# A graph network layer: edge sums kept transposed, and the node's own part multiplied in the edge stage

## What is computed

```python
h = jnp.maximum(_layernorm(x, axis=-1), 0.0)
# inside the first layer, with self loops of zero edge attributes added:
e = jax.nn.relu(ea @ ee_w1 + ee_b1) @ ee_w2 + ee_b2
msg = x[src] + e
agg = jax.ops.segment_sum(msg, dst, num_segments=n)
h = (1.0 + eps) * x + agg
h = jax.nn.relu(_ln(h @ w1 + b1, g1, be1))      # 256 -> 1024
h = jax.nn.relu(_ln(h @ w2 + b2, g2, be2))      # 1024 -> 1024
y = h @ w3 + b3                                 # 1024 -> 256
```

## Time and profile before

| | |
|---|---|
| median of 3 runs | 3159.45 us (3154.38 to 3160.02) |
| span of the profiled execution | 3157.3 us |
| block prepare | 0 to 93.0 us |
| block edges0 | 93.0 to 1107.8 us |
| block nodes, its steady part | 1250 to 2020 us |
| mean granted TensorE clock | 0.906 |

### The profile page before, as it was taken

How to read it: one execution, slowest core, us unless ns; L and a number is a source line. 1 busy time by engine, 2 the same in 40 slices (tenths; PEclk the granted TensorE clock), 3 DMA queues, 4 the chain that set the end, 5 groups by cost and what they waited for, 6 DMA issues and landing times. The chain is left out here.

```text
span 3157.3 us, 79016 instructions
## 1 busy us (share of the span) xinstructions
PE 2446.9 (77%) x25310; PEld 2164.9 (69%) x25311; DVE 2156.6 (68%) x3833; ACT 1488.6 (47%) x3803; POOL 1976.9 (63%) x2143
## 2 busy tenths in 40 slices
PE   0577777777777789999999999947777777777763
PEld 0466666666666679999999999945555555555552
DVE  7676667777677636666666666657766766666666
ACT  5444444444444458888888888831111111111114
POOL 4677777777777634444444444437777777777772
PEclk9998889999899889999999999978888888887996
DMA  6555555555555500000000000026555655555554
GB/s 158 168 161 149 158 154 166 161 163 160 159 164 158 143 25 18 21 21 20 20 21 20 20 22 21 21 61 178 171 173 173 174 172 168 173 172 173 171 170 136
DMA packets 183839, 373.69 MB, mean 118 GB/s; under 512 B 42598, under 2 KB 93688, under 8 KB 183769
## 3 DMA queue, kind: packets, MB, share of 16 engines
q0 software_dynamic: 75552, 209.66, 23.5%
q1 hardware_dynamic: 107392, 162.37, 17.4%
q10 hardware_dynamic: 824, 0.87, 0.1%
HBM read 346.95 MB, written 25.80 MB: 118 GB/s over the span
## 5 line engine op out<-in xcount | busy, mean ns | idle before, releaser
L446 POOL DMA_INDIRECT rows<-tab_scratch,srcs x784 | 765.7, 977 | 238.7 <-issue 234.1
L1458 POOL DMA_INDIRECT a_rows<-tab_scratch,srcs x784 | 750.5, 957 | 251.7 <-issue 235.8
L1524 PE MATMUL sum_ps<-feat,a_hot 128*125 128x264 f32 x1960 | 601.5, 463 | 237.5 <-DVE feat L1616 121.0
L1524 PEld LDWEIGHTS sum_ps<-feat,a_hot 128*125 128x125 f32 x1960 | 417.4, 222 | 341.7 <-DVE feat L1616 133.9
L876 PE MATMUL z_ps<-ah,w 128*128 128x125 f16 x6400 | 553.8, 219 | 1.0 <-PEq L982 1.0
L876 PE MATMUL z_ps<-al,w 128*128 128x125 f16 x3200 | 542.7, 217 | 0.0
L876 PEld LDWEIGHTS z_ps<-ah,w 128*128 128x128 f16 x6400 | 489.5, 97 | 1.5 <-issue 1.4
L1468 ACT ACTIVATE feat<-d 128x32 f32<-128x32 f32 x196 | 44.9, 229 | 827.0 <-DVE d L1612 566.2
L500 PE MATMUL mlp_ps<-ewa,eab 128*128 128x256 f16 x788 | 203.5, 290 | 284.3 <-PEq L496 283.3
L478 ACT ACTIVATE rh<-mlp_ps 128x1024 f16<-128x1024 f32 x196 | 199.7, 1019 | 358.2 <-ACTq L477 347.7
L829 POOL TENSOR_TENSOR a<-a 128x500 f32<-128x500 f32 x100 | 124.4, 1244 | 372.1 <-POOLq L828 372.1
(11 more groups left out here) (211 smaller groups left out, 5422.8 us busy)
## 6 DMA issues: line engine op xcount, KB each, us to landing
ea<-edge_t SPq DMA_DIRECT2D x394, 128.0 KB
dstb<-dst_flat SPq DMA_DIRECT2D x98, 512.0 KB
rows<-tab_scratch,srcs POOLq DMA_INDIRECT x784
a_rows<-tab_scratch,srcs POOLq DMA_INDIRECT x784
tab_scratch<-prow SPq DMA_DIRECT2D x50, 128.9 KB
hx<-x SPq DMA_DIRECT2D x50, 125.0 KB
x_scratch<-x SPq DMA_DIRECT2D x50, 125.0 KB
hs<-tab_scratch SPq DMA_DIRECT2D x50, 125.0 KB
```

Source lines behind the costliest of these rows:

```text
L446: pool.indirect_dma_start(rows[:, b % DEEP, k, :], None, dram["tab0"], bass.IndirectOffsetOnAxis(ap=srcs[:, c:c + 1], axis=0),).then_inc(r ...
L1458: pool.indirect_dma_start(rows[:, b % DEEP, k, :], None, dram["tab1"], bass.IndirectOffsetOnAxis(ap=srcs[:, c:c + 1], axis=0),).then_inc(r ...
L1524: ins = pe.matmul(out[:], hot[:, h, k, :], feat[:, row, k, :], start=(k == 0), stop=(k == CB - 1))
```

## The change

`acc` is kept transposed: features in the 128 partitions, and for each tile four blocks of 125 columns, two of the node's features and two of the edge activations.

In edges0 the operands of the sums trade places: the gathered rows and `rh`, `rl` become the weights and `hot` is streamed, 32 products of 125 columns in place of 16 of 256. `hot` is built by four TENSOR_SCALAR instructions of 125 columns from a float16 row in SBUF in place of one SCALAR_TENSOR_TENSOR of 500 columns with its row in PSUM. Once in four batches SP loads one tile's own rows of `tab0` back (`load_own`), PE transposes them with four products into `own_ps`, and DVE adds them, times (eps + 2), to `acc` (`add_own`). PE's loop covers 12 batches in place of 6.

In prepare `own` is gone; `acc` is filled with constants by two POOL copies of 6250 columns and two ACT instructions of 6250 columns, the normalised x goes to another buffer, and ACT's order of `high` and `normalised` is changed.

In nodes `turn`, `turned`, `turnable` and the two identity products are gone. `make_h` is four products that read `acc` directly; it stands behind the first layer. DVE adds the node's own part (`add_own`, into the new SBUF tile `hs`), and `high_h` and `low_h` read `hs` in place of PSUM.

```diff
@@ prepare
             for c in range(CH):
                 pool.wait_ge(norm_ready, c + 1)
                 if c >= 2:
-                    pool.wait_ge(t_free, c - 1)
+                    pool.wait_ge(tb_ready, c - 1)
@@ prepare, ACT
-            for c in range(CH + 2):
-                if c >= 2:
-                    high(c - 2)
+            for c in range(CH + 1):
                 if c < CH:
                     deviation(c)
+                if c >= 1:
+                    high(c - 1)
+                if c < CH:
                     normalised(c)
@@ prepare, DVE
-            for c in range(CH + 2):
-                if c >= 2:
-                    low(c - 2)
-                if 1 <= c < CH:
-                    own(c - 1)
+            for c in range(CH + 1):
                 if c + 1 < CH:
                     stats(c + 1)
+                if c >= 1:
+                    low(c - 1)
+                if c + 1 < CH:
                     coefficients(c + 1)
-            own(CH - 1)
@@ edges0
-    at = dsts[:, bass.ds(CB * (b + 1), CB)].unsqueeze(2).broadcast_to([P, CB, TN])
-    return dve.scalar_tensor_tensor(out=out, in0=at, scalar=negbase[:, bass.ds(tile, 1)],
-                                    in1=iota_ps.unsqueeze(1).broadcast_to([P, CB, TN]),
-                                    op0=ALU.add, op1=ALU.is_equal)
+    for k in range(CB):
+        ins = dve.tensor_scalar(out[:, k, :], iota16[:], dsts[:, bass.ds(CB * (b + 1) + k, 1)], negbase[:, bass.ds(tile, 1)],
+                                ALU.subtract, ALU.is_equal)
@@ edges0, PE
+                    node = hot[:, h, k, :]
+                    for f in range(KD):
+                        pe.matmul(mine, rows[:, ring, k, hi], node, start=(k == 0 and f == 0), stop=False, skip_group_check=True)
+                        pe.matmul(mine, rows[:, ring, k, lo], node, start=False, stop=False, skip_group_check=True)
+                        pe.matmul(edge, rh[:, s, k, hi], node, start=False, stop=False, skip_group_check=True)
+                        ins = pe.matmul(edge, rl[:, s, k, hi], node, start=False, stop=(k == CB - 1 and f == KD - 1), skip_group_check=True)
@@ nodes, PE
+                    for k in range(KD):
+                        edge = acc[:, bass.ds(i, 1), (KD + k) * TN:(KD + k + 1) * TN].rearrange("p a c -> p (a c)")
+                        ins = pe.matmul(h_ps[:, j, :], w2e[:, k, f], edge, start=(k == 0), stop=(k == KD - 1))
@@ nodes, ACT
-                act.wait_ge(h_done, 1)
-                act.sem_inc(h_done, -1)
-                act.activation(hh[:], h_ps, ACT.Copy, scale=1.0 / WS).then_inc(hh_ready, 1)
+                act.wait_ge(hs_ready, 1)
+                act.sem_inc(hs_ready, -1)
+                act.activation(hh[:], hs[:], ACT.Copy, scale=1.0 / WS).then_inc(hh_ready, 1)
@@ nodes, DVE
+            def add_own(i):
+                dve.wait_ge(h_done, 1)
+                dve.sem_inc(h_done, -1)
+                mine = acc[:, bass.ds(i, 1), 0:KD * TN].rearrange("p a c -> p (a c)")
+                dve.tensor_tensor(hs[:].rearrange("p k n -> p (k n)"), h_ps.rearrange("p k n -> p (k n)"), mine, ALU.add).then_inc(hs_ready, 1)
...
-                dve.scalar_tensor_tensor(out=hl[:], in0=h_ps, scalar=1.0 / WS, in1=hh[:],
+                dve.scalar_tensor_tensor(out=hl[:], in0=hs[:], scalar=1.0 / WS, in1=hh[:],
                                          op0=ALU.mult, op1=ALU.subtract).then_inc(h_split, 1)
```

More of the change, by code:

```diff
@@ L168, in _ @@
                 for rows in splits:
-                    sp.dma_start(acc[rows, tiles(c), 0:D], x_v[rows, tiles(c), :]).then_inc(ld_x[c], 16)
+                    sp.dma_start(xbuf(c)[rows], x_v[rows, tiles(c), :]).then_inc(ld_x[c], 16)
             sp.dma_start(sb["srcs"][:], t["src_cols"]).then_inc(stored, 16)
@@ L516, in _ @@
             edge_mlp(0)
+            pe.wait_ge(ident_ready, 1)
+            own()
             def body(tiles, i, u):
@@ L520, in body @@
                 edge_mlp(1 - s)
+                if u % RING == 1:
+                    own()
                 lo, end = tiles[u]
@@ L531, in body @@
                         pe.sem_inc(xhot_ready, -1)
-                        sums(sum_ps[:, 2, :], 2, u, s).then_inc(xsum_done, 1)
+                        sums(sum_ps[:, 2, :], 2, u % DEEP, s).then_inc(xsum_done, 1)
             with pe.Fori(0, FULL) as i:
-                tiles = tiles_of(nc, PE, table, DEEP * i, DEEP)
-                for u in range(DEEP):
-                    body(tiles, i, u)
-            tiles = tiles_of(nc, PE, table, DEEP * FULL, REST)
+                for half_round in range(2):
+                    tiles = tiles_of(nc, PE, table, ROUND * i + DEEP * half_round, DEEP)
+                    for u in range(DEEP):
+                        body({DEEP * half_round + u: tiles[u]}, i, DEEP * half_round + u)
+            tiles = tiles_of(nc, PE, table, ROUND * FULL, REST)
             for u in range(REST):
@@ L615, in _ @@
             low_parts(0)
+            add_own(NT - 1)
             def turn(i):
@@ L714, in nodes @@
         z_ps = [m.ps(f"z{j}_ps", [P, 2, 512]) for j in (1, 2)]
-        tv_ps = m.ps("tv_ps", [P, 3, TN])
-        hv_ps = m.ps("hv_ps", [P, 3, TN])
+        vv_ps = m.ps("vv_ps", [P, 2, TN])
+        h_ps = m.ps("h_ps", [P, KD, TN])[:]
         y_ps = m.ps("y_ps", [P, D])
         gp_ps = m.ps("gp_ps", [P, 512])
-        t_ps, h_ps, v_ps = tv_ps[:, 0:KD, :], hv_ps[:, 0:KD, :], [hv_ps[:, KD, :], tv_ps[:, KD, :]]
+        v_ps = [vv_ps[:, j, :] for j in range(2)]
         g_ps = gp_ps[:, 0:KD * TN].rearrange("p (k n) -> p k n", n=TN)
@@ L969, in body @@
                     layer1(1, range(3, 4))
+                if has(i, 0, 1):
+                    make_h(i + 1)
                 if has(i, 4):
@@ L1076, in body @@
             def body(i, p):
-                if has(i, 0, 1):
-                    turned(i + 1)
                 if has(i, 0):
@@ L1243, in body @@
                 if has(i, 0):
-                    inverse(0, v1_read if has(i, 0, 1) else None)
+                    inverse(0)
                 if has(i, 3):
```

210 lines of the change are left out of this document (108 added, 102 removed).

## The result

| | before | changed |
|---|---|---|
| median | 3159.45 us | 3309.72 us (3304.62 to 3311.61) |
| ratio | | 1.0478 (95%: 1.0464 to 1.0493) |
| span of the profiled execution | 3157.3 us | 3309.8 us |
| first to last of POOL's gathers in edges0 | 94.1 to 1097.4: 1003.3 | 100.8 to 1200.7: 1099.9 |
| last gather of edges0 to first of edges1 (nodes) | 1017.2 | 1063.0 |

The change costs 150 us. The three stages take +6.7 (all before the first gather), +96.6 and +45.8 us; the profiled spans differ by 3.4 more, behind the first gather of edges1, in code that did not change. I had forecast +44: +6, +9 and +29.

A forecast was written before the change was run, and what follows sets the result against it. POOL's indirect DMA gathers were taken to bound edges0, PE the nodes, and a chain of waits prepare. Nodes +29, edges0 +9 and prepare +6 made +44 on the 3159.45 us median: 3203 us, range 3183 to 3225.

The forecast's parts named there:

- The step that failed: edges0: the added PE, DVE and SP work hides behind POOL while DVE and PE stay under 5.2 us a batch.
- Two sizes in the same part: edges0: four `hot` instructions of 0.2 add DVE 0.1 us a batch or less; 50 own-row additions at about 0.42.
- Rival D: edges0 is the larger loss, by `hot` costing POOL as L547 does or PE refetching its loop; 3243, chance 0.07.
- PE has 270 us of air: edges0: PE's spare time, named against PE losing time by refetching instructions in its longer loop.
- six batches of slack: edges0: POOL's slack, named against the edge stage becoming the larger loss.
- The port term, +9,: edges0: new `hot`, SBUF to SBUF, lengthens POOL's issues by 0.009 for each of 984; +9 us, bounds 0 and +37.
- Nodes, +29 forecast: nodes: `low_h` with two SBUF inputs waits for POOL's L829; 0.60 a tile over 48 tiles, bounds -32 and +68.
- the removed products: nodes: two transposes and two identity products gone from PE, worth 0.67 a tile.
- Prepare, +6 forecast: prepare: ACT's new order starts the last rows at 85.3, not 79.13; +6 us, bounds 0 and +10.

The follow-up runs named there:

- experiment 5: Changed kernel with PE's edges0 loop back at 6 batches and without the own rows in edges0 (no load, products or addition): 3236.51 us, ratio 1.0246.
- experiment 6: Changed kernel, PE's edges0 loop of 6 batches, no own rows in edges0, `hot` again one instruction with its row in PSUM: 3205.35 us, ratio 1.0142.
- experiments 1: Changed kernel with PE's loop in edges0 back to 6 batches by an inner loop of two halves, same work and order: 3282.21 us, ratio 1.0386.
- experiment 7: Changed kernel with PE's edges0 loop of 6 batches and `hot` as one SCALAR_TENSOR_TENSOR with its row in SBUF: 3242.26 us, ratio 1.0259.
- experiment 8: Kernel before with the new four-instruction `hot` and one more DVE instruction of 250 columns in each fourth batch of edges0: 3221.17 us, ratio 1.0183.
- experiment 3: Kernel before with PE's loop of 24 batches instead of 6, nothing else changed: 3160.80 us, ratio 1.0004.
- experiment 9: Changed kernel with `h` kept in PSUM in nodes: own part added into `h_ps` in place, `high_h` and `low_h` read PSUM: 3279.47 us, ratio 1.0379.
- experiments 4: Kernel before with the new `hot`, four TENSOR_SCALARs from a float16 row in SBUF, nothing else: 3184.04 us, ratio 1.0071.

## Why the prediction was wrong

**The step that failed** is in the edges0 part: "All of this hides behind POOL as long as DVE and PE stay under POOL's 5.2 us a batch." I took DVE's 718 busy of 1015 us as 300 us of air and costed the new `hot` and `add_own` on DVE at nothing. DVE's gaps are no air. It works in turn with PE and ACT within a batch, and most of its idle time in edges0, 254 of 296 us, is waits for them: for the high parts of the edge attributes (L547) and of the activations (L579), both ACT's, and for PE's sums (L556). Of the kernel before, as totals with number of waits and the longest:

```profile
DVE eab L547 <- DVEq L546: 122.8, 80, 3.6
DVE acc L556 <- DVEq L554: 102.2, 68, 5.0
DVE rl L579 <- DVEq L578: 29.2, 39, 2.5
```

Two pairs of runs that differ in `hot` alone, and have no refetch on DVE, show that its time costs. Between experiments 5 and 6, without the own rows, 66 us of work cost 31. Between experiments 1 and 7, beside the own rows, 64 cost 40, or 55 by POOL's wait. In the changed kernel DVE was 794 us busy of 1112, still far from full. The own rows cost 44, as experiment 5 shows; that DVE's part in them is what costs is argued and not shown, since experiment 8 has the refetch in it and PE's four products weren't tried alone.

A part of each price may be the lower clock. PE's granted clock has two levels in these traces, full (1.00) and half (0.50). Two products of 125 columns start 0.10 us apart in a stretch at 0.50, and 0.05 apart in one at 1.00:

```profile
600.21 0.31 PE L526 MATMUL sum_ps<-hot,rows 128*128 128x125 f16 x1
600.31 0.31 PE L527 MATMUL sum_ps<-hot,rows 128*128 128x125 f16 x1
...
605.15 0.22 PE L526 MATMUL sum_ps<-hot,rows 128*128 128x125 f16 x1
605.20 0.22 PE L527 MATMUL sum_ps<-hot,rows 128*128 128x125 f16 x1
```

Added up over all products between the first and the last gather, the lower level lengthened PE's work by about 106 us in the changed kernel and 82 in the one before; experiments 1, 5 and 6 have 113, 92 and 83. So some 24 of the 97 us could have come by this way. No run held the clock, and whether it falls because PE is kept waiting, or PE's partners are late because it falls, is open.

**Two sizes in the same part.** The four small instructions take about 1.0 together, not 0.8: 243.5 us for 984, which put 68 us on DVE, some 0.3 a batch and not 0.1. And `add_own` is 0.47, not 0.42.

**Rival D** had the stage right and both reasons in a shape that does not hold. `hot` did not cost POOL as L547 does (978 against 977). The refetch is real, 133 packets, but experiment 3 has it at no price. It costs 27 us only beside the rest of the change. I had named both "PE has 270 us of air" and "six batches of slack" against it; only the second held, and only while DVE could catch up. D's chance of 0.07 was far too low, as was its price of 40.

**The port term, +9,** should have been 0. The means are 977 before and 978 after. The form of `hot` that does reach POOL's issues is the one with two SBUF inputs, 976 to 997 in experiment 7. The Trainium skill, "SBUF — State Buffer", section "Who interferes with whom", counts tensor_scalar among the forms that can take the shared ports, and infers that tensor_tensor, with two inputs, leaves descriptor generation alone. The runs show the reverse of what I had drawn from it: no effect of this tensor_scalar that can be seen, and a clear one of a two-input form. Here the measurement decides.

**Nodes, +29 forecast, +45.8 measured.** The mechanism is the one forecast, and experiment 9 shows it: 0.60 a tile from the collision. The period was nearly right, 19.65 against 19.71, with luck: two sizes offset each other, for the removed products are worth 0.48 and not 0.67, and PE's wait is 1.13 and not 1.27. 48 x 0.66 = 32 of the 45.8 are the steady tiles. The other 14 lie at the block's ends: from the last gather to the first `hh` it is 25.4 us where it was 17.7, and the rest is in the first tiles. Without the own rows and with the old `hot` those 25.4 are 16.4 (experiment 6). So these 7.7, about half of the 14, are edges0's lag carried over.

**Prepare, +6 forecast, +6.7 measured, by another way.** I held that ACT's first rows, 4 us later, would be covered by the wait for a stored slot. They start at 26.34, 7.6 later than in the earlier trace rows, and that wait is gone: the rows of ACT follow at 6.71 from there without it, and the last start at 86.95, 7.8 after 79.13. From the first rows to the last it is 60.6 us where it was 60.4. So it is the delay that arrives, and the new order of `high` adds next to nothing to it; no run takes the two apart. DVE's casts show where the delay comes from, one held by each of POOL's two copies:

```profile
8.49 5.50 DVE L263 CAST iota<-icol 128x125 f16<-128x125 int32 x1 [0.24 <-DVEq L252]
14.13 5.17 DVE L264 CAST negbase<-ineg 128x50 f32<-128x50 int32 x1
```

## What to carry to other kernels

Busy share is not slack. An engine that works in turn with others within an iteration can be at 70% and have little time to give. Look at who ends its waits, and if it is its partners in the ring, give added work a price: here 66 us of it cost 31, and 64 cost 40 where more had been added beside it. A stall that a deep buffer swallows (here 5 us at a loop's back edge) comes back as soon as the stages behind it can't catch up, so an edit that is free alone can be dear beside another. Compare the instruction queues of an experiment too, engine by engine: two runs here, made to isolate DVE's work, brought a refetch on DVE of their own. And move work to a stage in which its engine is idle: the own rows cost 44 us in edges0, and with them in prepare, in place of POOL's fills, prepare became 5.8 us shorter.

## What the hardware showed

- PE's loop of 24 batches of the old form, or of 12 of the new one, was fetched anew in each round (103 and 133 packets on the instruction queue; 27 to 30 with shorter loops), at about 3 us more for a back edge (5.50 against the 2.4 to 3.0 of a table load alone).
- DVE's loop was fetched anew in experiments 4 and 8 alone (100 and 99 packets where the others have 43 to 46), and DVE idled 23.9 and 47.0 us in 11 rounds ahead of its first instruction, 2.2 and 4.3 each.
- A DVE instruction with two SBUF inputs waits for a running POOL instruction that reads SBUF: 0.99 against 0.42 at the same place, with nothing changed but `hs` in SBUF or PSUM.
- A DVE instruction with two SBUF inputs lengthened those of POOL's indirect DMA issues that began within 0.5 us of its start (1.45 in place of 0.94; 976 to 997 ns on the mean with 246 of them), and, of those with no other DVE work beside them, none that had begun first. 984 short float16 TENSOR_SCALARs left the mean at 978.
- 125 columns of float16 in a TENSOR_SCALAR cost DVE 0.25 us each (243.5 / 984), 500 columns in one instruction 0.73.
